# The first 25 score rows of an attention layer as two 128-column matmuls each

## The chip, the cores and the metric

The kernel runs on one core of one Trainium2 chip. The metric is the device time of one execution in microseconds; for the kernel before it is the median of three runs. One more execution, the profiled one, was recorded by the hardware profiler, and all rows below are from it.

## The reference

A transformer layer on `x` of shape (2, 1024, 1024). After a layer norm the attention (weights reduced to signs, one scale per output channel) and a gated feed-forward network (4-bit weights with scale and zero point per group of 128) both work on the normalised input, and both are added to `x`:

```python
xn = _layernorm(x)
q = bitnet_linear(xn, q_weight, q_scale)   # 32 heads of 32
k = bitnet_linear(xn, k_weight, k_scale)   # 8 heads of 32, each for 4 query heads
v = bitnet_linear(xn, v_weight, v_scale)
scores = jnp.einsum('bhqd,bhkd->bhqk', q, k) / np.sqrt(HEAD_DIM)
attn = jax.nn.softmax(scores, axis=-1)
out = jnp.einsum('bhqk,bhkd->bhqd', attn, v)
x = x + bitnet_linear(out, o_weight, o_scale) + ffn(xn)
```

## The kernel before, in words

The program is written for each engine by hand, in a fixed order, with semaphores between the engines. No scheduler moves anything.

**Projections** (`project`, L1439). The 2048 positions are four chunks `c` of 512, and each has 12 output tiles `p` of 128 channels. One projection is 16 matmuls of 128 rows by 128 columns against 512 positions: 8 tiles of the input width, each with a high and a low fp16 part. ScalarE reads the result out of PSUM (L746), makes a mask (L753) and a high half (L759); VectorE clamps (L1077), repairs (L1081) and, for query and key tiles, makes the low half (L1094, in `tail`, from p = 3 on for the tile before).

**Attention** works in 32 units `u` (one key head of one batch and half of the queries), with 16 score rows each, 512 in all. A *score row* `i` is 128 queries against 1024 keys and is computed only to find each query's maximum. `row_scores(i, half)` (L1414) computes 128 queries against 512 keys into one of three PSUM banks, `c % 3`; `row_max` on VectorE (L1103) reduces each half to one column. The half `c` may be written when half `c - 3` has been reduced (the wait on `max_ok`). The contraction is 96 rows (three parts of 32). The 128 queries are split into four matmuls with 32 stationary columns each, and each lands in its own 32 partitions of the bank.

Behind the projections the loop over the 512 steps `e` interleaves row scores of row `e + 25`, `key_scores` (L1464, scores with the keys on the partitions, for the exponentials), `values` (L1478) and `pair_sums` (L1493). All four have 32 stationary columns per matmul. `maxima_rows` (L1422), once a unit, is a transpose of 128 columns in and 16 out.

**The early rows.** The exponentials of unit 0 need its maxima before attention begins, so 25 rows (`LEAD = 25`) are computed among the last projections:

```python
EARLY_ROWS = [(2, p, h) for p in (10, 11) for h in range(2)] + [(3, p, h) for p in range(9) for h in range(2)] + [(3, p, 0) for p in range(9, 12)]
```

A row (c, p, 0) stands in the middle of projection (c, p), after 8 of its 16 matmuls, and (c, p, 1) behind it. `EARLY` is 25 as well, so all 25 stand there and the loop for rows from `EARLY` to `LEAD` is empty. On VectorE both rows of a projection are reduced first, then its output is clamped and repaired; unit 0's maxima are joined by `top_max` (L1107) in projection (3, 5).

**Behind attention** come the output projection (L1610) and the feed-forward network (L1639, L1655) with its additions.

Of the kernel before, what the change touches and what calls it, by code (L numbers as in the profile page):

```python
# [5 lines left out]
P = 128  # L6
# [16 lines left out]
LEAD = 25  # L23
# [108 lines left out]
def layer_kernel(nc, x, wq, sq, wk, sk, wv, sv, wo, so, gw, gz, gs, uw, uz, us, dw, dz, ds, out, zscr, wscr, yscr, kscr, vscr, rscr):  # L132
# [7 lines left out]
    with ctx:  # L140
# [12 lines left out]
        def view(zone, kb, words, dt=f32):  # L153
            v = zone[:, kb * 256:kb * 256 + words]
            return v if dt == f32 else v.bitcast(dt)
# [30 lines left out]
        qst = [view(zone_b, kb, 1024, f16).rearrange("p (h c) -> p h c", h=4) for kb in (0, 4, 20)]  # L186
# [71 lines left out]
        ps = ctx.enter_context(nc.psum_tensor("ps", [P, 8, 512], f32))  # L258
# [1116 lines left out]
        def _(pe):  # L1375
            MM = nc.tensor.matmul
# [26 lines left out]
            def row_scores(i, half):  # L1403
                u = i // 16
                if i % 16 == 0 and half == 0:
                    pe.wait_ge(s[f"q_in{u % 3}"], 192 * (u // 3 + 1))
                    if u % 2 == 0:
                        pe.wait_ge(s[f"k_in{u // 2 % 2}"], 48 * (u // 4 + 1))
                c = 2 * i + half
                if c >= 3:  # L1410
                    pe.wait_ge(s["max_ok"], c - 2)
                for a in range(4):
                    c0 = i % 4 * P + 32 * a
                    last = MM(ps[32 * a:32 * a + 32, c % 3, :], qst[u % 3][0:96, i % 16 // 4, c0:c0 + 32],  # L1414
                              kst[0:96, u // 2 % 2, half * 512:(half + 1) * 512], start=True, stop=True)
                last.then_inc(s["s_pe"], 1)

# [6 lines left out]
            def project(c, p):  # L1424
                n, b2, s2, f = 12 * c + p, c // 2, c % 2, channels(c, p)
                if c == 0:
                    wait_weights(pe, p)
                if p == 0:
                    pe.wait_ge(s["xh_out"], 4 * (c + 1))
                    pe.wait_ge(s["xl_out"], 4 * (c + 1))  # L1430
                if n == 46:
                    pe.wait_ge(s["v_out"], 2 * (NC - 1))
                elif n == 47:
                    pe.wait_ge(s["mrow_ok"], 1)
                if output_before(n) is not None:
                    pe.wait_ge(s["y_ok"], output_before(n) + 1)
                for kt in range(KT):
                    for part in range(2):
                        last = MM(ps[:, output_bank(n), :], wT[:, kt, f * P:(f + 1) * P],  # L1439
                                  xT[:, b2, part, kt, s2 * 512:(s2 + 1) * 512],  # L1440
                                  start=(kt == 0 and part == 0), stop=(kt == KT - 1 and part == 1))
                    if kt == 3:
                        for r in early_row(c, p, 0):
                            row_scores(r, 0)
                            row_scores(r, 1)
                last.then_inc(s["qkv_pe"], 1)
# [89 lines left out]
            for c in range(NC):  # L1536
                i = 4 * (c + 1)
                for p in range(12):
                    project(c, p)
                    if c == 0 and p < 9:  # L1540
                        for k in ((2, 3), (4, 5), (6, 7), (8,), (9,), (), (10,), (), (11,))[p]:
                            turn_weights(k)
                    if p == (3 if c else 4):
                        turn_values(c)
                    if c + 1 < NC:
                        if p == 6:
                            pe.wait_ge(s["v_out" if c else "v0_out"], 2 * c if c else 2)
                            turn_high(i)
                        elif 7 <= p < 10:
                            turn_low(i + p - 7)  # L1550
                            turn_high(i + p - 6)
                        elif p == 10:
                            turn_low(i + 3)
                    for r in early_row(c, p, 1):
                        row_scores(r, 0)
                        row_scores(r, 1)
                    if (c, p) == (3, 7):
                        pe.wait_ge(s["v_out"], 2 * (NC - 1))
                        maxima_rows(0)
# [8 lines left out]
            for e in range(STEPS):  # L1568
                u, k = e // 16, e % 16
# [151 lines left out]
```

## Time and profile before

| | us |
|---|---|
| median of three runs (lowest, highest) | 2363.05 (2362.56, 2366.21) |
| profiled execution, its own time | 2364.19 |
| its span in the trace | 2362.1 |
| TensorE busy with matmuls | 2305.1 (98% of the span) |
| VectorE busy | 1802.5 (76%) |
| ScalarE busy | 1581.5 (67%) |
| GpSimd busy | 967.6 (41%) |
| row scores, all 4096 matmuls, TensorE busy | 407.5 |

The span is cut by the trace into instructions of each engine with their start and length, and a wait is put down to the instruction that ended it. Matmuls overlap in the pipeline: one of 128x512 is shown with about 0.38 us, while the next begins some 0.22 us after it. For what a matmul costs, starts are compared with starts.

### The profile page before, as it was taken

What the parts mean: (1) busy time and instruction counts of PE and PEld (TensorE: products, weight loads), DVE (VectorE), ACT (ScalarE), POOL (GpSimd) and SP (SyncE); (2) the same over time, 40 slices, a digit from 0 to 9 for tenths busy, and PEclk for the clock granted to TensorE, in tenths of its full rate; (3) what the DMA queues carried; (4) which work ended last, traced back from release to release, by engine and by line L of the source; (5) the groups of instructions that cost most, each with busy time, mean ns of one, the idle gap of its engine ahead of it and who ended that gap; (6) DMA issues with size and microseconds to landing.
All of it is one profiled execution on the core that took longest, in us unless ns stands there. A gap on an engine that the chain in (4) does not pass through costs nothing.

```text
span 2362.1 us, 45029 instructions
## 1 busy us (share of the span) xinstructions
PE 2305.1 (98%) x18561; PEld 1020.5 (43%) x18561; DVE 1802.5 (76%) x2314; ACT 1581.5 (67%) x2050; POOL 967.6 (41%) x531
## 2 busy tenths in 40 slices
PE   6999999999999999999999999999999999999998
PEld 3443344444444444434444444444444444444444
DVE  7878888888888888846577777777777777777777
ACT  5774788888888888872266666666665666666664
POOL 0000599999999999980022222210002222221000
PEclk9999999999999999999999999999999999999999
DMA  5130466555666655663211111131124111114111
GB/s 184 36 100 5 82 92 97 90 92 89 91 90 99 91 90 90 88 116 112 90 36 36 36 36 36 52 110 36 36 72 143 36 36 36 36 50 182 36 36 72
DMA packets 179905, 175.52 MB, mean 74 GB/s; under 512 B 87586, under 2 KB 127394, under 8 KB 179702
## 3 DMA queue, kind: packets, MB, share of 16 engines
q1 hardware_dynamic: 117430, 150.62, 20.5%
q0 software_dynamic: 62272, 22.03, 12.3%
q8 instruction: 147, 2.41, 0.4%
q14 instruction: 56, 0.46, 0.1%
HBM read 160.08 MB, written 65.45 MB: 95 GB/s over the span
## 4 chain that ended last, share of the span: by engine, by line
PE 53%; DVE 1%; issue 0%; ACT 0%; DVEq 0%
PE ps L1639 33%; PE ps L1655 16%; PE ps L1610 4%; PE ps L1671 0%; DVE zone L1355 0%; DVE xT L1355 0%; PE ps L1523 0%; DVE sm L1248 0%; ACT zone L922 0%; DVE zone L1065 0%; DVE zone L1066 0%; DVE zone L1259 0%; DVEq L140 0%; ACT zone L862 0%; DVE zone L1069 0%
## 5 line engine op out<-in xcount | busy, mean ns | idle before, releaser
L1639 PE MATMUL ps<-xT,zone 128*128 128x512 f16 x3584 | 774.6, 379 | 2.7 <-DVE zone L1355 2.7
L1103 DVE TENSOR_REDUCE zone<-ps 128x1 f32<-128x512 f32 x1024 | 639.2, 683 | 142.0 <-PE ps L1414 138.1
L779 ACT ACTIVATE zone<-ps,sm 128x512 f32<-128x512 f32 x1024 | 623.9, 698 | 144.8 <-PE ps L1464 144.2
L605 POOL TENSOR_TENSOR zone<-zone 128x1024 f32<-128x1024 f32 x252 | 643.9, 2687 | 135.8 <-ACT zone L779 102.8
L1332 DVE TENSOR_SCALAR ps<-ps,zone_c 128x1024 f32<-128x1024 f32 x392 | 506.7, 1293 | 160.8 <-PE ps L1639 158.7
L903 ACT ACTIVATE ps<-ps,zone_c 128x1024 f32<-128x1024 f32 x392 | 426.6, 1088 | 259.9 <-PE ps L1639 259.9
L1639 PEld LDWEIGHTS ps<-xT,zone 128*128 128x128 f16 x3584 | 350.2, 98 | 426.3 <-DVE zone L1355 4.2
L1464 PE MATMUL ps<-zone 98*32 98x512 f16 x4096 | 408.4, 380 | 4.2 <-ACT zone L779 3.8
L1414 PE MATMUL ps<-zone 96*32 96x512 f16 x4096 | 407.5, 381 | 4.5 <-issue 2.5
L1655 PE MATMUL ps<-zone 128*128 128x512 f16 x1792 | 387.1, 379 | 0.0
L1343 DVE TENSOR_SCALAR ps<-ps,zone_c 128x1024 f32<-128x1024 f32 x216 | 279.2, 1293 | 93.1 <-PE ps L1655 92.9
L651 POOL CAST zone<-zone 128x1024 f16<-128x1024 f32 x56 | 58.1, 1037 | 703.5 <-DVE zone L1336 703.5
L917 ACT ACTIVATE ps<-ps,zone_c 128x1024 f32<-128x1024 f32 x216 | 235.1, 1088 | 137.8 <-PE ps L1655 137.8
L1478 PE MATMUL ps<-zone 128*32 128x512 f32 x2048 | 268.6, 595 | 2.6 <-ACT zone L779 0.7
L1655 PEld LDWEIGHTS ps<-zone 128*128 128x128 f16 x1792 | 175.4, 98 | 211.4
L1464 PEld LDWEIGHTS ps<-zone 98*32 98x32 f16 x4096 | 117.7, 96 | 180.4 <-ACT zone L779 80.8
L1414 PEld LDWEIGHTS ps<-zone 96*32 96x32 f16 x4096 | 115.3, 96 | 180.1 <-DVE zone L1103 76.9
L1439 PE MATMUL ps<-xT,zone 128*128 128x512 f16 x768 | 180.3, 390 | 3.0 <-ACT xT L683 3.0
L659 POOL TENSOR_TENSOR xT<-xT,zone 128x1024 f32<-128x1024 f32 x8 | 18.7, 2355 | 361.8 <-ACT zone L922 361.8
L1493 PE MATMUL ps<-zone 128*32 128x512 f32 x1024 | 133.2, 592 | 0.4 <-DVE zone_c L1114 0.4
L653 POOL TENSOR_TENSOR zone<-zone 128x1024 f16<-128x1024 f32 x56 | 119.1, 2127 | 4.5
L1439 PEld LDWEIGHTS ps<-xT,zone 128*128 128x128 f16 x768 | 74.1, 100 | 97.7 <-issue 21.5
(137 smaller groups left out, 1331.5 us busy)
## 6 DMA issues: line engine op xcount, KB each, us to landing
zone<-dequantised SPq DMA_DIRECT2D x84, 512.0 KB, 3.6
dequantised<-zero_points SPq DMA_DIRECT2D x84, 256.0 KB, 4.3
zone<-zone SPq DMA_DIRECT2D x384, 32.0 KB, 2.4
zone<-_attn_hidden_states_dram SPq DMA_DIRECT2D x16, 512.0 KB, 6.4
zone<-inverse_sums SPq DMA_DIRECT2D x128, 64.0 KB, 2.5
attention<-zone SPq DMA_DIRECT2D x32, 256.0 KB, 2.0
xT<-attention SPq DMA_DIRECT2D x4, 2048.0 KB, 12.0
dequantised<-in_L_ffn_gate_w_dram POOLq DMA_DIRECT2D x28, 256.0 KB, 6.3
```

The costliest lines, as they stand in the source:

```text
L605: nc.gpsimd.tensor_tensor(duo[n % 3], prob[:, prob_slot(e), :], prob[:, prob_slot(e + 2), :], add).then_inc(s["sum_ok"], 1)
L779: A(prob[:, prob_slot(e), m % 2 * 512:(m % 2 + 1) * 512], ps[:, 3 + m % 3, :], ACT.Exp, scale=gam[:, 0:1]).then_inc(s["exp_ok"], 1)
L903: A(pair, pair, ACT.Copy, scale=tab[:, t, 0, g:g + 1]).then_inc(s["act_ok"], 1)
L1103: V.tensor_reduce(mxs[:, u % 2, half, i % 16:i % 16 + 1], ps[:, (2 * i + half) % 3, :], AX, amax).then_inc(s["max_ok"], 1)
L1332: V.tensor_scalar(pair, pair, tab[:, t, 1, g:g + 1], None, mult).then_inc(s["dve_ok"], 1)
L1343: V.tensor_scalar(pair, pair, dtab[:, it, o:o + 1], None, mult).then_inc(s["dve_ok"], 1)
L1414: last = MM(ps[32 * a:32 * a + 32, c % 3, :], qst[u % 3][0:96, i % 16 // 4, c0:c0 + 32], kst[0:96, u // 2 % 2, half * 512:(half + 1) * 512 ...
L1439: last = MM(ps[:, output_bank(n), :], wT[:, kt, f * P:(f + 1) * P], xT[:, b2, part, kt, s2 * 512:(s2 + 1) * 512], start=(kt == 0 and part ...
L1464: last = MM(ps[32 * b:32 * b + 32, 3 + m % 3, :], kst[0:98, u // 2 % 2, kt * P + 32 * b:kt * P + 32 * b + 32], qst[u % 3][0:98, 2 * hp + a ...
L1478: last = MM(ps[32 * h:32 * h + 32, 6, :], vst[:, u // 2 % 2, kt, :], prob[:, prob_slot(2 * kt + h // 2), h % 2 * 512:(h % 2 + 1) * 512], s ...
L1639: last = MM(ps[:, 4 * s2 + 2 * m + c, :], ring[:, buf, m * H + g * P:m * H + (g + 1) * P], xT[:, hf, part, g, c * 512:(c + 1) * 512], star ...
L1655: last = MM(ps[:, 4 * s2 + 2 * m + c, :], ring[:, k % RING, (it % 4) * 512 + o * P:(it % 4) * 512 + (o + 1) * P], hT[:, it, part, c * 512: ...
```

## The change

A row below 25 is now two matmuls, one for each half, with 128 stationary columns that fill the whole bank; all other rows stay at four matmuls of 32 columns for each half. Data, waits, increments and order are the same.

```diff
                 c = 2 * i + half
                 if c >= 3:
                     pe.wait_ge(s["max_ok"], c - 2)
-                for a in range(4):
-                    c0 = i % 4 * P + 32 * a
-                    last = MM(ps[32 * a:32 * a + 32, c % 3, :], qst[u % 3][0:96, i % 16 // 4, c0:c0 + 32],
+                wide = P if i < LEAD else 32
+                for a in range(0, P, wide):
+                    c0 = i % 4 * P + a
+                    last = MM(ps[a:a + wide, c % 3, :], qst[u % 3][0:96, i % 16 // 4, c0:c0 + wide],
                               kst[0:96, u // 2 % 2, half * 512:(half + 1) * 512], start=True, stop=True)
                 last.then_inc(s["s_pe"], 1)
```

TensorE's order before, around the first early rows (L1439 is a projection, L1414 the row scores, L1400 a transpose of the input's low part):

```order
L1392 MATMUL ps<-id,zone 128x128 x8
L1439 MATMUL ps<-xT,zone 128x512 x8
L1414 MATMUL ps<-zone 32x512 x8
L1439 MATMUL ps<-xT,zone 128x512 x8
L1400 MATMUL ps<-id,zone 128x128 x8
L1414 MATMUL ps<-zone 32x512 x8
L1439 MATMUL ps<-xT,zone 128x512 x8
```

And the same place in the changed kernel, whose lines behind the edit are one higher:

```order
L1392 MATMUL ps<-id,zone 128x128 x8
L1440 MATMUL ps<-xT,zone 128x512 x8
L1415 MATMUL ps<-zone 128x512 x2
L1440 MATMUL ps<-xT,zone 128x512 x8
L1400 MATMUL ps<-id,zone 128x128 x8
L1415 MATMUL ps<-zone 128x512 x2
L1440 MATMUL ps<-xT,zone 128x512 x8
```

Nothing has moved: each early row has 2 instructions where it had 8, and they are as wide as their neighbours. The end of the projections before, where attention begins with `key_scores` (L1464):

```order
L1439 MATMUL ps<-xT,zone 128x512 x16
L1414 MATMUL ps<-zone 32x512 x8
L1439 MATMUL ps<-xT,zone 128x512 x8
L1464 MATMUL ps<-zone 32x512 x12
L1414 MATMUL ps<-zone 32x512 x4
L1464 MATMUL ps<-zone 32x512 x4
```

There the first of these L1414 groups, row 24, becomes two wide matmuls; the second, x4, is half a row of attention and stays. VectorE's order is the same in both kernels.

## Rows read from the trace of the kernel before

**Rows 1.** The page, busy time of each engine.

```profile
PE 2305.1 (98%) x18561; PEld 1020.5 (43%) x18561; DVE 1802.5 (76%) x2314; ACT 1581.5 (67%) x2050; POOL 967.6 (41%) x531
```

**Rows 2.** Windows: stretch, its length, busy us of each engine, clock.

```profile
183.42:247.93 64.51, 64.51 (x436) 23.73 (x435) 53.10 (x91) 27.37 (x42) 0.00 (x0) 1.00 0.09 30
214.00:240.00 26.00, 26.00 (x175) 9.28 (x172) 23.28 (x42) 10.98 (x18) 0.00 (x0) 1.00 0.00 1
300.00:1000.00 700.00, 695.81 (x9845) 286.67 (x9841) 575.70 (x1006) 575.86 (x978) 677.88 (x354) 1.00 0.60 92
1090.00:2343.00 1253.00, 1250.16 (x5838) 570.36 (x5837) 925.66 (x790) 751.48 (x698) 189.66 (x119) 1.00 0.17 58
```

**Rows 3.** Timeline of TensorE, projections without score rows: start, us, instruction.

```profile
107.42 1.04 PE L1453 MATMUL ps<-id,zone 128*128 128x128 f32 x8
108.29 10.52 PE L1439 MATMUL ps<-xT,zone 128*128 128x512 f16 x48
118.65 0.61 PE L1392 MATMUL ps<-id,zone 128*128 128x128 f16 x8
119.10 1.24 PE L1439 MATMUL ps<-xT,zone 128*128 128x512 f16 x5
```

**Rows 4.** Timeline of TensorE among the early rows.

```profile
183.42 0.61 PE L1414 MATMUL ps<-zone 96*32 96x512 f16 x8
...
195.76 0.78 PE L1414 MATMUL ps<-zone 96*32 96x512 f16 x8
196.48 1.90 PE L1439 MATMUL ps<-xT,zone 128*128 128x512 f16 x8
...
225.34 0.61 PE L1414 MATMUL ps<-zone 96*32 96x512 f16 x8
225.89 1.90 PE L1439 MATMUL ps<-xT,zone 128*128 128x512 f16 x8
227.72 0.62 PE L1414 MATMUL ps<-zone 96*32 96x512 f16 x8
...
230.10 0.61 PE L1414 MATMUL ps<-zone 96*32 96x512 f16 x8
230.65 0.28 PE L1422 MATMUL ps<-id,zone 128*16 128x128 f32 x1
230.76 1.89 PE L1439 MATMUL ps<-xT,zone 128*128 128x512 f16 x8
...
247.93 0.83 PE L1464 MATMUL ps<-zone 98*32 98x512 f16 x12
```

**Rows 5.** Timeline of TensorE, attention at its steady pace.

```profile
900.90 0.39 PE L1414 MATMUL ps<-zone 96*32 96x512 f16 x4
901.12 0.39 PE L1464 MATMUL ps<-zone 98*32 98x512 f16 x4
```

**Rows 6.** Timeline of VectorE among the early rows.

```profile
186.70 1.29 DVE L1103 TENSOR_REDUCE zone<-ps 128x1 f32<-128x512 f32 x2 [1.54 <-PE ps L1414]
...
191.46 1.29 DVE L1103 TENSOR_REDUCE zone<-ps 128x1 f32<-128x512 f32 x2 [0.42 <-PE ps L1414]
...
195.41 2.48 DVE L1103 TENSOR_REDUCE zone<-ps 128x1 f32<-128x512 f32 x4
...
225.80 1.29 DVE L1103 TENSOR_REDUCE zone<-ps 128x1 f32<-128x512 f32 x2 [0.20 <-PE ps L1414]
...
228.85 1.28 DVE L1103 TENSOR_REDUCE zone<-ps 128x1 f32<-128x512 f32 x2
230.55 1.29 DVE L1103 TENSOR_REDUCE zone<-ps 128x1 f32<-128x512 f32 x2 [0.43 <-PE ps L1414]
```

**Rows 7.** Timeline of TensorE, start of attention.

```profile
256.21 0.39 PE L1464 MATMUL ps<-zone 98*32 98x512 f16 x4
258.55 0.40 PE L1414 MATMUL ps<-zone 96*32 96x512 f16 x4 [1.95 <-DVE zone L1103]
...
259.37 0.56 PE L1464 MATMUL ps<-zone 98*32 98x512 f16 x4
...
263.01 0.39 PE L1414 MATMUL ps<-zone 96*32 96x512 f16 x4
```

**Rows 8.** Windows of TensorE there: length, busy, granted clock.

```profile
261.00:262.00 1.00, 1.00 (x8) 0.50 0.00 0
```

## The prediction, made before the changed kernel was run

> **What bounds the kernel now.** I read the page first: TensorE is busy for 98% of the span, VectorE for 76% [rows 1]. Such shares are means, so I then asked the windows for the stretch that the change touches. From the first early row (183.42) to the first `key_scores` (247.93) TensorE is busy for all of its 64.51 us, and VectorE for 53.10. In the part where each projection brings two score rows as well as a low half for VectorE (214 to 240) it is 26.00 of 26 against 23.28 [rows 2]. TensorE sets the pace, with VectorE at 90% right behind it. What follows is bound by TensorE too: 695.81 of 700 us in attention and 1250.16 of 1253 behind it [rows 2]. So a microsecond that TensorE saves among the early rows moves all later work, as long as nothing else was the pace there.
>
> A busy engine need not be a useful one, so the next view is the timeline, read from start to start. Without score rows, 48 matmuls of 128x512 take 118.65 - 108.29 = 10.36 us, or 0.216 each [rows 3]. In attention a group of four 32-column matmuls also takes 901.12 - 900.90 = 0.22 us [rows 5]: the four run beside each other and cost no more than one wide matmul. If streaming were all, the change would be worth nothing. But among the early rows the groups and the wide matmuls alternate, and there the starts don't add up. From 225.34 to 227.72 are 2.38 us, for 2 groups and 8 wide matmuls, which are 10 x 0.216 = 2.16. 0.22 is left over: 225.89 - 225.34 = 0.55 for two groups instead of 0.43 is 0.12 on leaving the narrow form, and 227.72 - 225.89 = 1.83 for eight instead of 1.73 is 0.10 on entering it [rows 4].
>
> Is it the change of width? Where wide matmuls follow wide transposes there is none of it: eight transposes of 128x128 take 119.10 - 118.65 = 0.45, and eight of the values 108.29 - 107.42 = 0.87, with no remainder in the 48 matmuls between [rows 3]. `maxima_rows` (128 in, 16 out) behaves like a wide one: the step from narrow to it costs the 0.12 (230.10 to 230.65), and from it to the projection only 0.11 pass in all [rows 4]. In attention, narrow stays behind narrow and nothing is left over [rows 5]. The whole stretch agrees: 64.51 less 266 slots of 0.216 (216 projection matmuls and 50 groups, 57.4), less 0.45 and 0.87 for the two sets of transposes, 0.11 for the maxima and a wait of 0.17 (below) leaves 5.5 us, for 50 switches: 0.11 each.
>
> **The change part by part.** *Instructions.* 50 groups of four become 50 wide matmuls: 200 matmuls and 200 weight loads less 150 of each. A wide matmul on 96 rows is in no row of before. From below its slot is 0.216, as a narrow group on 96 rows or a wide matmul on 128 rows; from above it is 0.39, the whole length that a narrow group is shown with [rows 5], if none of it overlapped. I take 0.216, since both its width and its row count stand in rows at that slot. So this edit costs 0 on its own; the upper bound would cost 50 x 0.174 = 8.7 us.
>
> *Fewer instructions by themselves.* The groups in attention show that eight narrow instructions fit into two slots, so the six that go per row are worth nothing by that row. The Trainium skill puts an overhead of some 60 cycles on each matmul (TensorEngine Tiling (Array Packing), Instruction Overhead): as an estimate from that page, 150 fewer at 2.4 GHz would give 3.75 us beside the switches, 8.8 in all. The slot of the narrow groups speaks against it.
>
> *Switches.* All 25 rows stand alone between wide work, so 50 switches were paid. One of the stretch's 50 stays (the last projection to `key_scores`), and the entry at 183.42 goes as well: 50 x 0.11 = **-5.5 us**.
>
> *VectorE's answer.* The work of VectorE is the same, and the score banks tie it to TensorE: half 1 of a row waits until half 0 of the row before is reduced. This wait is real once before: the row at 195.76 is shown with 0.78 in place of 0.61, a wait of 0.17 [rows 4], for the reduction at 195.41 [rows 6]. VectorE is late there because two low halves stand back to back. How much earlier does it come now? At 191.46 it waited 0.42 for TensorE, and the point before that ties it is 186.70, also a wait for TensorE [rows 6], which comes 3 switches (0.33) earlier. So VectorE comes 0.33 + 0.42 = 0.75 earlier, and TensorE by 11 switches, 1.21. Half 1 is held by VectorE before and now, so it moves by 0.75 only: **+0.46**, and the wait grows from 0.17 to 0.63.
>
> From there VectorE has air (three projections without a low half), until p = 3. Then a projection with its two rows costs VectorE 4.32: from 225.80 to 230.55, less 0.43 idle [rows 6]. TensorE needs 4.75 now, and 20 slots, 4.32, after the change. It is a tie. What counts is the slack at (3, 7, 1), the tightest point: its half 1 starts at 230.10 + 0.22 = 230.32, and the reduction it needs ends at 228.85 + 0.68, with some 0.07 for the signal at 229.60. Of this 0.72, four switches take 0.44, and VectorE's lag the rest: `top_max` in (3, 5) costs it about 0.23 (its idle falls from 0.43 to 0.20 at 225.80 [rows 6]), and a rounding of 0.01 to 0.02 a projection. About nothing is left over, and about nothing is lost: 0 to 0.4 us, I take **+0.05**. VectorE's idle of 0.2 to 0.4 in each round goes, and its busy share from p = 4 to 8 rises from 90% to over 97%.
>
> *Start of attention.* It begins when TensorE comes out of the last projection, and all of it moves. The row (3, 11, 0) is the last to lose a switch; VectorE was waiting for TensorE behind it. The maxima's DMA into the query tile follows TensorE's own transpose, so it moves nearly as far.
>
> Sum: -5.5 + 0.46 + 0.05 = **-5.0 us**. The profiled execution would go from 2364.19 (span 2362.1) to 2359.2 (span 2357.1). It was 1.1 above the median of 2363.05, and against that I predict **2358.0**.
>
> **Rivals.**
>
> *The clock's dip goes or stays.* At 256.2 to 258.55 TensorE stands still (1.95 us, for VectorE), and from about 259.4 to 263.0 its granted clock is at 0.50, the 1.2 GHz level [rows 7, 8]. The 3.64 us between the starts at 259.37 and 263.01 would be about 1.8 at the full level, so the dip costs up to 1.8. Everything comes 5 us earlier now, and whether a still stand of this length is answered with a dip may depend on when it falls. Without it: 2358.0 - 1.8 = 2356.2. Against it: the still stand itself is untouched by the edit. Chance 0.18.
>
> *VectorE becomes the bound.* If its round is really a tenth longer than TensorE's 4.32, or the bank's release comes later than my 0.07, the six rounds from p = 3 to 8 each give back 0.1 to 0.3, with the known 0.46 in all 1 to 2.5 us: 2358.6 to 2360.1, in the middle 2359.6. For it speaks the tie above, against it the slack that I count. Chance 0.22.
>
> *The change doesn't do what it says.* The left-over belongs to something other than width (to the change of operand tile or of the PSUM bank from projection to scores), and stays: 2363. Against it are the transposes, which change operand and bank without it [rows 3]. Chance 0.06.
>
> *Slower.* The wide matmul on 96 rows doesn't pipeline, and its slot is 0.39 or more. The switches are worth 0.11 a half, so it decides from a slot of 0.33 up. At 0.39, where TensorE is too slow to wait for VectorE, the sum is 8.7 - 5.5 = +3.2: 2366.3. Over 0.2% needs a slot of 0.42, about half rate. Nothing shows a wide form at such a price. Chance 0.04.
>
> The forecast itself, dip kept and VectorE just keeping up, has 0.50.
>
> **How the numbers follow.** 0.2% of 2363 is 4.7 us, about what a measurement of this kernel can tell from no change, and the forecast of 5.0 lies at this line. Its own range is 2357.2 to 2359.0; over half of it, 0.30, is below 2358.3. With the case without the dip (0.18) and a little of the second (0.04) that is 0.52 for faster. Slower by over 0.2% has 0.03, the same 0.45. The range takes in the case without the dip, the second, and the runs' own scatter: 2355.8 to 2361.0.
>
> **What would show each step.** In the profile after, L1415's first 50 matmuls have 128 columns, the starts from row to row are 2.16 in place of 2.38, and the leave and entry remainders are gone. The row (3, 0, 1) starts its half 1 about 0.6 late. The first `key_scores` starts near 242.9. VectorE's waits for L1415 between the rows shrink from 0.4 to under 0.1. The dip is at about 254.4 to 258, or gone. I am wrong if row spacing stays over 2.3, if waits of TensorE for L1103 appear in each round, or if the 5 us at 243 are not there at the end of the span.

## The result, and the profile after

| | before | after |
|---|---|---|
| median of 10 runs (lowest, highest), us | 2363.91 (2361.21, 2370.85) | 2358.39 (2355.96, 2359.38) |
| profiled execution, span, us | 2362.1 | 2356.2 |
| TensorE busy, us | 2305.1 | 2298.3 |

The ratio is 0.9975 with a 95% interval of 0.9966 to 0.9984: 5.9 us less, between 3.8 and 8.0. The same kernel measured again (`wide_again` below) came to 0.9979, 0.9970 to 0.9988, or 5.0 us less. The medians themselves lie 5.5 and 5.8 us apart.

The timeline of TensorE after, at the places of [rows 4] (start, us, instruction):

```profile
183.20 0.60 PE L1415 MATMUL ps<-zone 96*128 96x512 f16 x2
...
194.46 0.38 PE L1415 MATMUL ps<-zone 96*128 96x512 f16 x1
195.24 0.39 PE L1415 MATMUL ps<-zone 96*128 96x512 f16 x1 [0.40 <-DVE zone L1103]
195.46 1.89 PE L1440 MATMUL ps<-xT,zone 128*128 128x512 f16 x8
...
221.85 0.60 PE L1415 MATMUL ps<-zone 96*128 96x512 f16 x2
222.29 1.89 PE L1440 MATMUL ps<-xT,zone 128*128 128x512 f16 x8
224.01 0.60 PE L1415 MATMUL ps<-zone 96*128 96x512 f16 x2
...
226.18 0.60 PE L1415 MATMUL ps<-zone 96*128 96x512 f16 x2
226.61 0.27 PE L1423 MATMUL ps<-id,zone 128*16 128x128 f32 x1
226.72 1.89 PE L1440 MATMUL ps<-xT,zone 128*128 128x512 f16 x8
...
242.80 0.83 PE L1465 MATMUL ps<-zone 98*32 98x512 f16 x12
```

A slot is the 0.216 us from the start of one wide matmul to the next. Two halves take 222.29 - 221.85 = 0.44, eight projection matmuls 224.01 - 222.29 = 1.72, a row with its half projection 2.16: ten slots and nothing over. The step into the maxima's transpose (226.18 to 226.61) is free too. The stretch from the first row to the first key scores is 242.80 - 183.20 = 59.60 us, 64.51 before. The one loss that grew is the row at 194.46: its half 1 waits for VectorE.

The weight loads (LDWEIGHTS, shown as PEld) show where the left-over stood. Before, on the way out of a row (matmul at 225.89) and at the entry into the next (matmul at 227.72):

```profile
225.89 1.41 PEld L1439 LDWEIGHTS ps<-xT,zone 128*128 128x128 f16 x8 [0.42 <-issue]
227.72 0.12 PEld L1414 LDWEIGHTS ps<-zone 96*32 96x32 f16 x8 [0.42 <-issue]
```

and after, for the matmuls that start at 221.85, 222.07 and 222.29:

```profile
221.64 0.10 PEld L1415 LDWEIGHTS ps<-zone 96*128 96x128 f16 x1
221.94 0.10 PEld L1415 LDWEIGHTS ps<-zone 96*128 96x128 f16 x1 [0.20 <-DVE zone L1103]
222.07 1.61 PEld L1440 LDWEIGHTS ps<-xT,zone 128*128 128x128 f16 x8
```

Among wide matmuls a load starts up to 0.22 ahead of its matmul (0.13 for the one that waits for VectorE), so its 0.10 us are hidden. At both changes of width before, load and matmul start together. The 0.10 to 0.12 us that a change costs is about one load; that the exposed load is the whole price is an argument from these starts, and no run tests it.

VectorE after (the places of [rows 6]):

```profile
189.26 2.58 DVE L1103 TENSOR_REDUCE zone<-ps 128x1 f32<-128x512 f32 x4
...
193.83 0.75 DVE L1094 SCALAR_TENSOR_TENSOR zone<-zone,sm 128x512 f16<-128x512 f32 x1 [0.16 <-ACT zone L759]
194.50 2.48 DVE L1103 TENSOR_REDUCE zone<-ps 128x1 f32<-128x512 f32 x4
...
221.20 2.48 DVE L1103 TENSOR_REDUCE zone<-ps 128x1 f32<-128x512 f32 x4
...
225.43 2.48 DVE L1103 TENSOR_REDUCE zone<-ps 128x1 f32<-128x512 f32 x4
```

Before, the reductions of a projection's two rows stood apart but for 195.41, as two pairs with a wait for TensorE ahead of the second. Now most run as four (2.48 us without a gap, up to 2.66 with a short one); in the first projection with rows and in the three without a low half they still stand apart. Four in a row take less than two pairs, so a whole round of VectorE is 225.43 - 221.20 = 4.23 us. From 210 to 234 VectorE is busy for 23.07 us of 24. In the same windows view, behind the still stand at the start of attention (length, busy, granted clock, DMA), the clock is whole where [rows 8] had 0.50:

```profile
253.00:254.00 1.00, 0.59 (x8) 1.00 0.00 0
254.00:255.00 1.00, 1.00 (x20) 1.00 0.00 0
```

Where the 5.9 us between the two spans come from, by the starts in the timelines and in the chain that ended last:

| stretch | before | after | difference |
|---|---|---|---|
| to the first early row | 183.42 | 183.20 | -0.2 |
| to the first key scores | 64.51 | 59.60 | -4.9 |
| to the first `pair_sums` | 18.18 | 17.04 | -1.1 |
| to the output projection | 822.58 | 821.55 | -1.0 |
| to the feed-forward network | 84.39 | 84.39 | 0 |
| to the end | 1189.0 | 1190.4 | +1.4 |

Only the second row is the edit's own, with 0.1 of the first (the entry into the first row). The third is the clock. The others are no larger than the scatter from one profile to the next: over all kernels below the first row starts between 181.1 and 183.4, and the stretch from `pair_sums` to the output projection takes 820.0 to 824.4 in those that leave attention as it is. The +1.4 at the end lies wholly behind the last instruction of the chain: from there to the end of the span are 5.0 us before and 6.4 after, and 4.9 to 6.1 in the kernels below that leave attention as it is.

### The profile page after: what moved, and what is told of

It reads as the page before. It is cut to its first block, busy times and chain, and to the rows that moved or that the text cites. A ratio compares the mean times of both kernels' runs of the same rounds, so it can differ in the third digit from the quotient of the medians.

```text
span 2356.2 us, 44729 instructions
## 1 busy us (share of the span) xinstructions
PE 2298.3 (98%) x18411; PEld 1026.5 (44%) x18411; DVE 1802.8 (77%) x2314; ACT 1580.2 (67%) x2050; POOL 966.0 (41%) x531
## 3 DMA queue, kind: packets, MB, share of 16 engines
q8 instruction: 146, 2.39, 0.4%
## 4 chain that ended last, share of the span: by engine, by line
PE 53%; DVE 1%; issue 0%; ACT 0%; DVEq 0%
PE ps L1640 33%; PE ps L1656 16%; PE ps L1611 4%; PE ps L1672 0%; DVE zone L1355 0%; DVE xT L1355 0%; PE ps L1524 0%; DVE sm L1248 0%; ACT zone L922 0%; DVE zone L1065 0%; DVE zone L1066 0%; DVE zone L1259 0%; DVEq L140 0%; DVE zone L1069 0%; DVEq L1068 0%
## 5 line engine op out<-in xcount | busy, mean ns | idle before, releaser
L1415 PE MATMUL ps<-zone 96*32 96x512 f16 (+1 forms) x3946 | 407.9, 380 | 4.9 <-issue 2.6
L1415 PEld LDWEIGHTS ps<-zone 96*32 96x32 f16 (+1 forms) x3946 | 117.9, 96 | 174.4 <-DVE zone L1103 76.2
```

Of the source, the lines that this page charges most:

```text
L1415: last = MM(ps[a:a + wide, c % 3, :], qst[u % 3][0:96, i % 16 // 4, c0:c0 + wide], kst[0:96, u // 2 % 2, half * 512:(half + 1) * 512], sta ...
```

## Experiments

**The changed kernel again, as yardstick.**

> The changed kernel once more, as the yardstick for the runs beside it. Every theory: 5.0 to 5.9 us below the kernel before, row spacing 2.16 us, first key scores 5.0 to 5.1 us earlier. Open: whether the stretch of half clock behind the still stand of 1.9 us is there; it was at 259.4 to 263 in the profile before and is in no row of the profile after. If it is only a matter of when the still stand falls, it should stay away here too; if it comes by chance, it may be back, and the span is then some 1.1 us longer.

Median 2357.23 beside 2363.03 before, ratio 0.9979. First row at 183.41, first key scores at 243.02: 59.61. No stretch of half clock.

**64 columns.**

```diff
-                wide = P if i < LEAD else 32
+                wide = 64 if i < LEAD else 32
```

> The early rows with two matmuls of 64 columns for each half: 4 instructions a row in place of 8, but still of another width than the projections. Switches of the tile width are the cause: nothing is gained, row spacing stays at 2.36 to 2.38 us, time within 1 us of the kernel before (perhaps less the half-clock stretch). Fewer instructions are the cause (rival): 4 of the 6 that the change removes are gone, so two thirds of the 0.22 us a row, spacing 2.23 us, 3.7 us gained. The step between 32-column tiles and full width is special (rival): anything between.

Median 2360.67, ratio 0.9993 (0.9985 to 1.0002). The median is 2.4 us below the kernel before, more than the 1 us that I had allowed, but the whole run can't tell a small gain from none; the timeline of TensorE can:

```profile
203.17 0.62 PE L1415 MATMUL ps<-zone 96*64 96x512 f16 x4
203.73 1.90 PE L1440 MATMUL ps<-xT,zone 128*128 128x512 f16 x8
205.56 0.62 PE L1415 MATMUL ps<-zone 96*64 96x512 f16 x4
```

With half of the instructions the row spacing is 205.56 - 203.17 = 2.39, and from the first row (181.09) to the first key scores (245.77) are 64.68 us, as before the change. Nothing is gained there, and the instruction count is ruled out. The width need not be 32: 64 columns among 128 pay the same. That its profiled span (2357.3) is nearly 5 us below the one before, with the changed stretch as long as ever, shows how far the rest of a run scatters: its first row stands 2.3 us earlier, and from `pair_sums` to the output projection it has 819.96.

**Full width with eight instructions.**

```diff
-                    last = MM(ps[a:a + wide, c % 3, :], qst[u % 3][0:96, i % 16 // 4, c0:c0 + wide],
-                              kst[0:96, u // 2 % 2, half * 512:(half + 1) * 512], start=True, stop=True)
+                    for k0 in range(0, 512, keys):
+                        last = MM(ps[a:a + wide, c % 3, k0:k0 + keys], qst[u % 3][0:96, i % 16 // 4, c0:c0 + wide],
+                                  kst[0:96, u // 2 % 2, half * 512 + k0:half * 512 + k0 + keys], start=True, stop=True)
```

with `keys` 128 for the early rows and 512 elsewhere.

> The early rows at 128 stationary columns, but each half as four matmuls of 128 keys: 8 instructions a row as before, all of full width. Switches are the cause: the whole gain stays, spacing 2.16 to 2.20 us, 5 to 5.9 us below the kernel before. Instruction count is the cause (rival): no gain, 2.38 us.

Median 2357.68, ratio 0.9982 (0.9973 to 0.9991). In the timeline:

```profile
202.54 0.61 PE L1416 MATMUL ps<-zone 96*128 96x128 f16 x8
202.99 1.89 PE L1441 MATMUL ps<-xT,zone 128*128 128x512 f16 x8
204.71 0.61 PE L1416 MATMUL ps<-zone 96*128 96x128 f16 x8
```

The spacing is 2.17, the stretch 241.91 - 181.93 = 59.98. The gain is there with as many instructions as before. Together the two runs separate width from count in both directions. This profile has the half-clock stretch (0.50 from 253 to 256).

**All rows wide.**

```diff
-                wide = P if i < LEAD else 32
+                wide = P
```

> All 512 score rows at 128 columns, also those inside attention, between 32-column key scores. Switches are the cause: four more switches in each of 487 steps, 487 x 4 x 0.11 = 214 us if all of it shows, so about 2570 us; the 0.22 us from one start to the next in attention become 0.33. Instruction count is the cause (rival): 2922 fewer matmuls and no loss, 2358 us or less.

One run, 2541.82 us. The timeline inside attention:

```profile
499.94 0.39 PE L1415 MATMUL ps<-zone 96*128 96x512 f16 x1
500.26 0.40 PE L1465 MATMUL ps<-zone 98*32 98x512 f16 x4
500.59 0.39 PE L1415 MATMUL ps<-zone 96*128 96x512 f16 x1
500.91 0.40 PE L1465 MATMUL ps<-zone 98*32 98x512 f16 x4
501.24 0.39 PE L1415 MATMUL ps<-zone 96*128 96x512 f16 x1
501.56 0.40 PE L1465 MATMUL ps<-zone 98*32 98x512 f16 x4
501.79 0.60 PE L1479 MATMUL ps<-zone 128*32 128x512 f32 x4
```

Four steps of 0.32 and 0.33 make 501.24 - 499.94 = 1.30, 0.325 each in place of 0.22 [rows 5], so a switch costs 0.106. From narrow to narrow (501.56 to 501.79) it is 0.23, as it was. From the first key scores to the output projection are 1023.6 us, 838.6 in the changed kernel: 185 more, or 0.095 for each of 1948 switches, where I had expected 214. The sign and the price at each place are as the switches say; about 29 us were overcounted. A unit takes 31.27 where it took 24.98, 6.29 more for 64 switches. The starts of one unit account for that: 64 x 0.106 is 6.78. The maxima's transpose takes off 0.24, since it stands beside wide work now. Short waits of the narrow unit take off 0.32 (0.09 behind 364.38 and 0.23 behind 374.24 in the changed kernel's timeline), which the wide unit does not have. That leaves 6.22.

**The clamp of the last projection into PSUM**, on the kernel before and after. In both profiles VectorE's clamp (L1077) takes 2.3 us in place of 0.42 while GpSimd adds, just ahead of the still stand. In the changed kernel:

```profile
249.26 2.38 POOL L605 TENSOR_TENSOR zone<-zone 128x1024 f32<-128x1024 f32 x1
249.62 2.29 DVE L1077 TENSOR_SCALAR zone<-zone 128x512 f32<-128x512 f32 x1
```

GpSimd's addition begins ahead of the clamp and ends at 251.64, the clamp at 251.91.

```diff
-                ch.inc(V.tensor_scalar(clamped, output(p), 1e6, -1e6, amin, amax))
+                held = ps[:, 7, :] if n == 12 * NC - 1 else clamped
+                ch.inc(V.tensor_scalar(held, output(p), 1e6, -1e6, amin, amax))
...
-                V.copy_predicated(output(p), mask.bitcast(i32), clamped).then_inc(s["r_ok"], 1)
+                V.copy_predicated(output(p), mask.bitcast(i32), held).then_inc(s["r_ok"], 1)
...
+                if u == 1:
+                    pe.wait_ge(s["r_ok"], 12 * NC)
```

The added wait keeps the next maxima out of PSUM bank 7 until the repair has read the clamped values there.

> The kernel before, but the last projection's clamp on VectorE (2.31 us beside GpSimd's first additions, 0.42 elsewhere) writes to a free PSUM bank instead of SBUF. If it is held up by GpSimd over SBUF, it takes 0.5 to 0.7 us in PSUM, the still stand of TensorE of 1.95 us behind it shrinks to 0.3 or less, and the half-clock stretch is gone: 1.5 to 3.4 us below the kernel before. If the form with a PSUM output is held as well, nothing changes.

> The same edit on the changed kernel. The difference to the same edit on the kernel before is then the switches alone, with no half-clock stretch in either: 5.0 us (-5.5 and 0.4 to 0.5 given back at the row that waits for VectorE). If the change's gain beyond 5.0 us came from the clock, the difference is 5.0 and not 5.9.

On the kernel before: 2362.20, ratio 1.0000 (0.9989 to 1.0012), and on the changed one 2358.36, 0.9983 (0.9974 to 0.9992). VectorE's timeline of `clamp_wide`:

```profile
249.26 0.68 DVE L1078 TENSOR_SCALAR ps<-zone 128x512 f32<-128x512 f32 x1
250.07 0.77 DVE L1082 COPY_PREDICATED zone<-zone_c,ps 128x512 f32<-128x512 int32 x1
250.72 2.47 DVE L1104 TENSOR_REDUCE zone<-ps 128x1 f32<-128x512 f32 x4
253.11 2.08 DVE L1095 SCALAR_TENSOR_TENSOR zone<-zone,sm 128x512 f16<-128x512 f32 x1
```

and TensorE's:

```profile
251.46 0.40 PE L1416 MATMUL ps<-zone 96*32 96x512 f16 x4 [0.35 <-DVE zone L1104]
255.85 0.40 PE L1416 MATMUL ps<-zone 96*32 96x512 f16 x4 [1.28 <-DVE zone L1104]
```

The clamp is free of the hold-up (0.68), but the low half behind it, which has two SBUF inputs and takes 0.74 elsewhere, isn't: it takes 2.08, to 255.19, and GpSimd's next addition beside it (252.27, 2.37 us long) ends at 254.64. The still stand of 1.95 has become 0.35 and 1.28. My expectation of 1.5 to 3.4 us failed: the wait moved by one instruction. The Trainium skill describes this (SBUF — State Buffer, Who interferes with whom): VectorE and GpSimd share one pair of SBUF ports, and whoever issues first holds it for its whole instruction, against a VectorE instruction in a two-port mode or one with two SBUF inputs while GpSimd reads SBUF. The 2.31, 0.68 and 2.08 us agree with it; no run here shows in which mode the clamp ran.

As a comparison of the switches alone the pair still serves. The stretch from first row to key scores is 246.92 - 182.41 = 64.51 in the one and 242.44 - 182.83 = 59.61 in the other, 4.9 apart, and the medians are 3.8 apart, where I had expected 5.0. But the kernel before had a half-clock stretch here too (from about 261.7 to 265.1, behind the shorter stand of 1.27), so I didn't get the pair without it.

**The maxima as a plain matmul.** In attention the transpose costs two switches each unit.

```diff
-                TR(ps[0:16, 7, 0:P], mtop, id32[:]).then_inc(s["m_pe"], 1)
+                MM(ps[0:16, 7, 0:P], mtop, id32[:], start=True, stop=True).then_inc(s["m_pe"], 1)
```

> On top of that, the transpose of the unit's maxima (128 rows in, 16 columns out, 31 times inside attention) becomes a plain fp32 matmul with the identity. As a transpose it behaves like full width: 0.10 us on entering and 0.09 on leaving, beside 0.11 of its own. As a plain matmul of 16 columns it should run as a narrow tile without switches, but with 0.21 to 0.23 us of its own: 31 x (0.30 - 0.22) = 2.5 us gained. If the left-over there isn't a switch, 31 x 0.11 = 3.4 us lost.

> The changed kernel with the maxima as a plain fp32 matmul with the identity, and nothing else. In the run before this, beside the clamp in PSUM, a unit of attention became 0.13 us shorter (24.98 to 24.85), because the other three column groups go on beside it: 31 x 0.13 = 4.0 us less than the changed kernel, about 2354. If that gain needed the clamp's edit, nothing.

With the clamp's edit 2352.96, ratio 0.9964 (0.9951 to 0.9976), without it 2355.49, 0.9961 (0.9947 to 0.9975). The changed kernel, once a unit:

```profile
357.29 0.43 PE L1465 MATMUL ps<-zone 98*32 98x512 f16 x4
357.65 0.28 PE L1423 MATMUL ps<-id,zone 128*16 128x128 f32 x1
357.86 0.40 PE L1415 MATMUL ps<-zone 96*32 96x512 f16 x4
358.09 0.39 PE L1465 MATMUL ps<-zone 98*32 98x512 f16 x4
```

and `maxmm` at the same place of another unit:

```profile
380.26 0.43 PE L1465 MATMUL ps<-zone 98*32 98x512 f16 x4
380.48 0.27 PE L1423 MATMUL ps<-id,zone 128*16 128x128 f32 x1
380.52 0.39 PE L1415 MATMUL ps<-zone 96*32 96x512 f16 x3
380.59 0.27 PE L1423 MATMUL ps<-id,zone 128*16 128x128 f32 x1
380.70 0.38 PE L1415 MATMUL ps<-zone 96*32 96x512 f16 x1
380.73 0.57 PE L1465 MATMUL ps<-zone 98*32 98x512 f16 x4
```

From key scores to key scores 0.80 became 0.47. The matmul (two passes in the trace) occupies one group of 32 columns, and the row's other three matmuls begin 0.04 us behind it. Part is paid back later in the unit by steps that are longer than 0.22 (0.28 behind 380.95 and 386.67, 0.35 behind 387.17, where the changed kernel has one of 0.31; one of 0.45 is in both), and a unit is shorter by 0.12 to 0.14 only (355.64 to 380.48 is 24.84, against 24.98 or 24.99). For 31 units that is 3.7 to 4.3 us, more than the 2.5 that I had expected first, since I hadn't counted on the overlap. Among the projections the same edit loses: unit 0's maxima stand between wide matmuls there, and the stretch from first row to key scores is 59.93 in place of 59.60. The ratios of these two kernels are below the ones without it, though their intervals overlap those of the changed kernel.

**The late low half.**

```diff
+                    if (c, p) == (NC - 1, 0):
+                        tail(NC - 2, 11)
...
-                if c + 1 < NC:
+                if c + 2 < NC:
                     tail(c, 11)
```

> The changed kernel with VectorE's low half of the last tile of chunk 2 moved behind the reductions of the first two rows of chunk 3. If the 0.4 us that the row (3, 0, 1) waits comes from the two low halves that stand back to back ahead of its reduction, the wait goes, and the stretch from the first row to the first key scores falls from 59.60 to 59.2 us. If the wait only moves to a later row, it stays at 59.6.

Median 2357.03, ratio 0.9972 (0.9960 to 0.9983). The wait at the row (3, 0, 1) is gone, no other row waits, and the stretch is 241.51 - 182.48 = 59.03, 0.57 less than in the changed kernel (I had expected 0.4 less). So the two low halves back to back were its cause. In the whole run it can't be told from the changed kernel.

**Both.**

> Both: 4.0 and 0.4 us less than the changed kernel, about 2353.5, and 9.5 below the kernel before.

Median 2353.30 beside 2363.94 before, ratio 0.9954 (0.9942 to 0.9967): 10.9 us less, span 2349.3. It has the lowest ratio of all kernels here.

## Why the prediction was right

**The number.** From 2363.05 I forecast 2358.0, and 2358.39 came. Part of that closeness is luck: over ten runs the kernel before stands at 2363.91, 0.9 higher, so the step is 5.5 by the medians and 5.9 by the ratio where I had 5.0. What follows rests on the stretch, not on the total. An interval of 0.9966 to 0.9984 also leaves open whether the kernel is faster by more than the 0.2% of which I wrote.

**The switches.** Predicted -5.5 for 50 of them. In the profile the ten slots of a row fill 2.16 exactly, and the stretch lost 4.9, with the entry ahead of it 5.0, after a given back 0.4: -5.4. `cols64` and `wide8` show that it is the width, `allwide` that it holds with the sign turned, at 0.106 a switch. The rival "doesn't do what it says" is out, and so is the one of fewer instructions: by the overhead of a matmul in the Trainium skill (TensorEngine Tiling (Array Packing), Instruction Overhead) I had estimated 8.8 us, switches included; `wide8` has none of the instructions removed and 59.98 against 59.60 for the stretch, so six instructions a row are worth at most 0.4 us in all.

**The wide slot on 96 rows.** Taken as 0.216 between bounds of 0.216 and 0.39: the profile has 0.44 for two. The slower rival is out.

**VectorE's answer.** The wait was put at the row (3, 0, 1), 0.63 long in place of 0.17. It is there: half 1 starts at 195.24, a slot behind 194.46 is 194.68, so 0.56. The term of +0.46 is 0.39. From p = 3 on no row waits; the +0.05 and the rival that gave it 1 to 2.5 us measured zero. But two steps of that count were off. VectorE's round is 4.23 and not 4.32, because I had taken it from two pairs of reductions, so it was no tie: VectorE gains 0.1 a round. And (3, 7, 1) is not the tightest point. Counted in the same way, from the reduction's end and signal to the start of half 1, (3, 6, 1) had 225.56 - 225.07 = 0.49 before, behind this reduction, where I had 0.72 for the other:

```profile
224.32 1.28 DVE L1103 TENSOR_REDUCE zone<-ps 128x1 f32<-128x512 f32 x2
```

After the change 222.07 - 221.95 = 0.12 is left there, and 0.22 at (3, 7, 1). At (3, 6, 1) the weight load of half 1 already waits for VectorE, until 221.94, and its matmul is just not late. VectorE's share there is 96%, I had said over 97.

**The first key scores** were put near 242.9 and start at 242.80; the sum of -5.0 is the 4.9 and 0.1 above. It stays in the span to the end.

**The clock.** The forecast case kept the half-clock stretch. The profile after shows the rival in which it goes, with the size wrong: from the key scores to the first `pair_sums` it is 18.18 with it and 17.04 without, 1.1 us, where I had put up to 1.8 by halving the whole time. The work that took 3.64 us (259.37 to 263.01) takes 2.23 after (254.23 to 256.46), 1.4 less, and 0.3 is lost again before `pair_sums`. Without it TensorE stands at other places for what it had won (0.20 for VectorE's `top_max`). It is not bound to the narrow rows alone: with a still stand of 1.94 to 1.96 us at this place it came in `before`, `cols64` (18.15) and `wide8` (17.97), and not in the changed kernel's two profiles, `maxmm`, `latetail` and `maxmm_latetail` (17.04 each time it was without, within 0.01). Counting the clamp's runs, it came in all three profiles with narrower early rows and in one of the eight in which just the early rows are 128 wide, so whether the edit makes it rarer is open. What decides it stays open; it is not the start alone, since `wide8` has it behind a stand that ends at 252.52 and `latetail`, at 252.12, has not. I can't say how often it comes in the timed runs. The difference of ratios between 5.9 and 5.0 us is no evidence for it, as both intervals hold both.

## What to carry to other kernels

Cost a tiled matmul by what stands on either side of it. A group of 32-column tiles costs as much as one wide matmul, and each change between widths cost 0.11 us here, so pick the width of the neighbours: wide among projections, narrow inside attention. Before taking a gain on the engine that bounds, replay the next engine's round beside the new pace: here VectorE had 4.23 us of work for a new round of 4.32, and only one row, where two low halves met, gave something back. For a gain of 0.2% read the stretch that was edited, since the rest of a run scatters by as much.

## What the hardware showed that was not expected

- Full-width matmuls change into 64-column tiles at the same price as into 32: a row spacing of 2.39 against 2.38.
- At a change of tile width the first weight load doesn't run ahead of its matmul: both start at 225.89, where among wide matmuls the load is 0.21 us ahead (221.64 for 221.85). In attention the same goes for the transpose (both at 357.65), and as a plain matmul its load is 0.22 ahead again (380.26 for 380.48).
- An fp32 transpose with 128 rows in and 16 columns out behaves like full width: free beside wide rows (226.18 to 226.61 for two slots), 0.14 us late behind narrow ones (357.29 to 357.65). The same product as a plain matmul behaves like a narrow tile (0.33 us lost among projections), and the next row's matmuls in the other three column groups run beside it.
- The time that GpSimd holds VectorE up is tied to the moment, not to an instruction: with the clamp out of the way the low half behind it took 2.08 us in place of 0.74. The held clamp ended 0.3 us and the held low half 0.6 us behind GpSimd's addition.
